# Moving the first layer's large loads behind the first placements of queries in a one-core transformer kernel

## What is computed

```python
xn = _layernorm(x)
# latent attention
q = xn @ wq ; k_lat = xn @ wk_down ; v_lat = xn @ wv_down
k = k_lat @ wk_up ; v = v_lat @ wv_up
y = softmax(causal(q @ k.T * 128**-0.5)) @ v ; a = y @ wo
# six layers
for i in range(6):
    h = attn_layer(shift_tokens(h), Wqkv[i], q_scale[i], k_scale[i], Wo[i]) + h
    h = ffn_layer(shift_tokens(h), ln_g[i], ln_b[i], W1[i], b1[i], W2[i], b2[i]) + h
out = x + a + h          # h starts as xn
```

## Time and profile before

| | us |
|---|---|
| median of 3 runs | 1826.56 (1821.57 to 1828.48) |
| the profiled execution, own time | 1832.16 |
| its span, first to last instruction | 1830.4 |
| TensorE busy | 1633.6 (89%) |
| VectorE busy | 1517.1 (83%) |
| ScalarE busy | 1312.9 (72%) |
| GpSimd busy | 1311.1 (72%) |
| mean granted TensorE clock | 0.975 |

### The profile page before, as it was taken

One profiled execution on the slowest core, in us unless ns is written; L12 is line 12 of the kernel. 1 busy time (PEld: TensorE's weight loads), 2 busy tenths in 40 slices (PEclk: granted clock), 3 DMA queues, 4 the chain that ended last, 5 costly groups with the idle time before them and its releaser, 6 DMA issues.

```text
span 1830.4 us, 72588 instructions
## 1 busy us (share of the span) xinstructions
PE 1633.6 (89%) x31192; PEld 1112.7 (61%) x31192; DVE 1517.1 (83%) x1941; ACT 1312.9 (72%) x1868; POOL 1311.1 (72%) x1287
## 2 busy tenths in 40 slices
PE   6777776788999999999999999999999999999995
PEld 5555665455656666666566666656666666666654
DVE  4466566689988999889899989989899998999973
ACT  2465564567788778777877887778777877887773
POOL 3100001888998888898789988889988899888871
PEclk7899999999999999999999999999999999999998
DMA  6011010010000100000100001000010000000000
GB/s 189 11 37 43 17 36 1 4 56 7 8 14 7 56 8 7 11 15 30 33 8 12 15 7 56 7 10 15 8 39 25 7 12 15 7 7 8 7 7 27
DMA packets 47997, 40.61 MB, mean 22 GB/s; under 512 B 33217, under 2 KB 41153, under 8 KB 46017
## 3 DMA queue, kind: packets, MB, share of 16 engines
q1 hardware_dynamic: 47680, 35.98, 7.0%
HBM read 20.22 MB, written 1.05 MB: 12 GB/s over the span
## 4 chain that ended last, share of the span: by engine, by line
PE 44%; issue 24%; DVE 17%; ACT 7%; POOL 6%; SPq 1%; DMA 0%; DVEq 0%; POOLq 0%; ACTq 0%
PE banks L1170 18%; PE banks L1444 10%; PE banks L1393 5%; PE banks L1468 5%; PE banks L1429 4%; DVE arena L1033 3%; DVE lnx L1095 3%; DVE small L1062 2%; DVE small L1068 2%; DVE small L1056 2%; DVE small L1080 1%; ACT L821 1%; ACT arena L755 1%; DVE arena L1028 1%; ACT L824 1%
## 5 line engine op out<-in xcount | busy, mean ns | idle before, releaser
L1444 PE MATMUL banks<-M,xs 128*32 128x512 f32 x3072 | 368.2, 597 | 0.6 <-ACT arena L755 0.3
L1028 DVE TENSOR_TENSOR arena<-banks,tabs 128x1024 f32<-128x1024 f32 x192 | 233.7, 1217 | 39.6 <-ACT arena L715 23.9
L514 POOL TENSOR_TENSOR arena<-arena 128x1024 f32<-128x1024 f32 x96 | 229.7, 2392 | 46.0 <-DVE arena L1033 45.7
L755 ACT ACTIVATE arena<-banks 128x1024 f32<-128x1024 f32 x192 | 196.9, 1025 | 71.1 <-PE banks L1444 69.8
L1033 DVE TENSOR_TENSOR arena<-banks,tabs 128x1024 f32<-128x1024 f32 x192 | 233.0, 1213 | 0.0
L519 POOL TENSOR_TENSOR arena<-arena 128x1024 f32<-128x1024 f32 x96 | 228.1, 2376 | 0.0
L509 POOL TENSOR_TENSOR prob<-prob,small 128x1024 f32<-128x1024 f32 x96 | 183.8, 1914 | 31.5 <-DVE small L1070 31.5
L1095 DVE SCALAR_TENSOR_TENSOR lnx<-lns,small 128x128 f32<-128x128 f32 x96 | 174.4, 1816 | 34.5 <-POOL small L562 33.5
L1170 PE MATMUL banks<-qkH,xsH 128*128 128x512 f32 x384 | 172.8, 450 | 32.3 <-DVE arena L1033 26.5
L1468 PE MATMUL banks<-arena 128*32 128x128 f32 x6144 | 192.3, 278 | 4.2 <-ACT arena L821 4.2
L574 POOL TENSOR_TENSOR arena<-arena,small 128x1024 f32<-128x1024 f32 x96 | 182.8, 1904 | 9.8 <-POOL arena L519 0.5
(11 more groups left out here) (127 smaller groups left out, 3727.0 us busy)
## 6 DMA issues: line engine op xcount, KB each, us to landing
arena<-in_wvo_dram SPq DMA_DIRECT2D x6, 1024.0 KB, 5.3
qkraw<-in_wqk_dram SPq DMA_DIRECT2D x6, 1024.0 KB, 5.3
gq<-w1w SPq DMA_DIRECT2D x64, 64.0 KB, 2.0
lns<-Xt SPq DMA_DIRECT2D x96, 32.0 KB
lns<-Xt SPq DMA_DIRECT2D x96, 31.8 KB
xsH<-w1w SPq DMA_DIRECT2D x32, 64.0 KB, 2.0
xsL<-w1w SPq DMA_DIRECT2D x32, 64.0 KB, 2.0
W<-in_w_dram SPq DMA_DIRECT2D x6, 341.0 KB, 3.2
```

Of the source, the lines that this page charges most:

```text
L514: pool.tensor_tensor(kc, kc, ks, ALU.add).then_inc(s["k_add"], 1)
L755: act.activation(vw[:, (2 * k + g) % RV, :], two(V_BANK), ACT.Copy).then_inc(s[f"v_cp{g}"], 1)
L1028: dve.tensor_tensor(heads(c), heads(two(0)), table(k % NT, kind), ALU.mult).then_inc(s[done], 1)
L1444: ins = pe.matmul(bk(V_BANK + z)[WIN * q:WIN * (q + 1), :], xs[:, b, t0:t0 + WIN], M[:, q, :, :].rearrange("p m n -> p (m n)"), start=True ...
```

## The change

The seven issues for layer 0 (`WVO0`, `qkraw`, scales, `tabc`, W1, W2, parameters) move behind `place_queries(0, 0)`, with its two waits and 16 DMAs. The table load comes after the scales now. The loads of W2 and of the parameters of layer 1 move behind `place_queries(0, 1)`. The other 6 calls of `place_queries` stay as they are, and so do the streams of the other four engines.

```diff
--- before.py
+++ after.py
@@ -321,8 +321,6 @@
             sp.dma_start(gwv, wvd).then_inc(lat_w, 16)
             sp.dma_start(gwo, wo.rearrange("(h p) n -> p h n", p=P)).then_inc(lat_w, 16)
             sp.dma_start(gwvu, wvuT).then_inc(lat_w, 16)
-            sp.dma_start(WVO0, wvo[0]).then_inc(wvo_in, 16)
-            sp.dma_start(tabc[:, :, :], tab_d).then_inc(tab_in, 16)
 
             def load_qk(l):
                 sp.dma_start(qkraw[:, :, :], wqk[l]).then_inc(qk_in, 16)
@@ -353,14 +351,6 @@
                 ahead_row = Xt[P - 1:P, n - 1, 64:D] if n % NT else zrow[:, :]
                 sp.dma_start(lns[0:1, f, 64:D], ahead_row).then_inc(rows_in[f], 16)
                 sp.dma_start(lns[:, f, 0:64], Xt[:, n, 0:64]).then_inc(rows_in[f], 16)
-
-            load_qk(0)
-            load_scales(0)
-            load_w1(0)
-            load_w2(0)
-            load_w2(1)
-            load_par(0)
-            load_par(1)
 
             def place_queries(it, z):
 
@@ -375,7 +365,18 @@
                         sp.dma_start(gQ[h][LAT * o:LAT * (o + 1), CH * z:CH * (z + 1)].bitcast(F32), part[LAT * h:LAT * (h + 1), :].bitcast(F32))\
                           .then_inc(gQ_in[h], 16)
 
-            for it in range(B * KV):
+            place_queries(0, 0)
+            sp.dma_start(WVO0, wvo[0]).then_inc(wvo_in, 16)
+            load_qk(0)
+            load_scales(0)
+            sp.dma_start(tabc[:, :, :], tab_d).then_inc(tab_in, 16)
+            load_w1(0)
+            load_w2(0)
+            load_par(0)
+            place_queries(0, 1)
+            load_w2(1)
+            load_par(1)
+            for it in range(1, B * KV):
                 for z in range(2):
                     place_queries(it, z)
             out_t = out.rearrange("b (t p) d -> p (b t) d", p=P)
```

## The result

The changed kernel takes 1846.87 us at the median of 4 runs (1841.94 to 1850.21), the kernel before 1827.52 in 4 runs, three of which are those that the forecast started from. The ratio is 1.0107, with a 95% interval of 1.0071 to 1.0143: slower by 1.1%, where 1844.1 us and +17.5 us had been forecast and 1837 to 1851 was the range. Timed again, 6 runs beside 17 of the kernel before, it was 1847.14 against 1829.99, ratio 1.0107 (1.0080 to 1.0134).

A forecast was written before the change was run, and what follows sets the result against it. The start follows its own chain of work: SyncE awaits the queries, TensorE runs in program order. First score +18.0 us, less 0.5 given back, is +17.5: 1826.56 + 17.5 = 1844.1 us, range 1837 to 1851.

The forecast's parts named there:

- What bounds the start: SyncE idles from 13.7 to 19.21 us awaiting the queries; earlier loads cost placements nothing at issue, only at landing.
- Placements: SyncE's first 16 placements still start no earlier than 19.21 us; their issue takes 10.3 us instead of 11.2.
- T0: Time when SyncE is free to issue WVO0: 29.5 us (29.2 to 30.4), where before it was issued at 9.00.
- The loads: From WVO0's issue until layer 0's parameters land: 13.0 us, bounds 12.2 and 14.5; landed at 42.5.
- TensorE: Products end at 40.0, hidden under the loads by 2.5 us; shifts take 2.3; first score at 44.8, +18.0 us.
- Given back: ScalarE's copy of the second query half no longer waits for placements: -0.5 us of the 0.96.
- GpSimd: Its preparation with tables and projection weights ends near 50 us, before a 243 us wait; costs nothing.
- The sum: Whole kernel: 18.0 - 0.5 = +17.5 us (16.4 to 19.9), 1844.1 us against the median, 1.0% slower.
- A: Rival: TensorE's clock rises sooner after the late start; price -7, giving +10.5, 1837.1 us; chance 0.10.
- B: Rival: loads land later or TensorE's clock stays lower; +19.9 to +22.4, 1849.0, up to 1851; chance 0.08.
- C: Rival: TensorE's scores overtake products and shifts, first score at 23.9; -3.4, 1823.2 us; chance 0.02.
- D: Rival: a resource with its own time sets later stages, so the end stays; 0 to -1, 1826; chance 0.02.

The follow-up runs named there:

- the run with its wait for placements: Changed kernel with WVO0, W1 and layer 0 parameters issued first and shifts(0) behind the first row's transposes: 1831.37 us against 1829.99, ratio 1.0006.
- half the dose: Changed kernel with only 8 placements (heads 0 and 1) ahead of the seven loads, those of heads 2 and 3 behind: 1848.86 us in one run.

## Why the prediction was right

*What bounds the start.* Right: SyncE's first placement stayed at 19.13, and no load had held it. That the loads ahead cost the placements something at landing (2.4 us at the median) is true of some, but not of the last, for which the copy waited: it landed in 1.98.

*Placements.* 10.1 us of issue instead of 10.3, T0 at 29.29 instead of 29.5. The reason given, a queue without loads, was not the right one: the 11.2 us of before come mostly from one issue of 1.45 us, and such an issue appears with the needed loads first too, when no load is left in the queue. Why it is absent in both profiles of the changed kernel is open.

*The loads.* The parameters landed at 32.79 + 8.65 = 41.4, that is 12.15 us after T0. The sum had 13.0 with bounds of 12.2 and 14.5. This was the term that was mis-sized most, by 0.85 us; the lower bound, made of loads one behind the other, was the true value. Nothing lay beside them. The upper end was the value with placements beside them: 14.0 and 14.2 us to the release in the two runs that have it.

*TensorE.* Right: `WVO0` landed at 34.5 (34.8), the products ended at 38.04 + 2.08 = 40.1 (40.0) and were covered, by 1.45 us instead of 2.5, since the load was shorter. The run with only the needed loads late showed what is behind the cover. From shifts to first score 2.27 us (2.3). First score +17.07 (18.0). The idle time began at 18.3 and not at 19.5, since `products(0, 0)`, which was part of the group at 16.64, left it with the change; that cost nothing. The sum comes out of two figures as well: `WVO0` started 20.3 us later, and the shifts started 12.3 us after its issue where they had started 15.5 us after it, so 3.2 us had been slack: 20.3 - 3.2 = 17.1.

*Given back.* 0.47 us (0.5), whole at the second block of transposes too: 49.87 - 43.84 = 6.03 us after the first score, 33.26 - 26.77 = 6.49 before. *GpSimd:* nothing (nothing), its split ended at 49.9 (near 50).

*The sum.* +16.83 at the first projection in the first profile, +20.5 in the second, +17.2 and +19.4 between medians, forecast +17.5. The forecast's 1844.1 lies 2.8 us below the 1846.87: 1.0 of it is the kernel before, at 1827.52 instead of the 1826.56 of the three runs that the forecast started from, and 1.8 is the difference. In the comparison with more runs it is the other way round: the kernel before is 3.4 us higher (1829.99) and the difference 0.3 smaller. That the medians agree so closely with +17.5 is in part luck, with runs of one kernel spread over some 13 us.

*The rivals.* A, the clock that rises sooner, did happen, but it was worth nothing in the end. In the kernel before the clock stayed at the lower level until 43.5, 16.7 us after the first score. In the changed kernel it was up from 49.6 us, 5.8 us after the first score, and down again at 53.0:

```profile
50.00:51.00 1.00, 1.00 (x8) 0.96 (x9) 0.26 (x1) 0.67 (x3) 0.87 (x2) 1.00 0.00 0
...
54.00:55.00 1.00, 1.00 (x7) 1.00 (x6) 0.00 (x0) 0.00 (x0) 0.00 (x0) 0.50 0.39 96
```

The last figures are the granted clock, the DMA's share and GB/s. The first of the products with the values, in the kernel before and in the changed kernel:

```profile
37.68 3.68 PE L1170 MATMUL banks<-arena 128*128 128x64 f32 x16 [1.70 <-DVE arena L949]
```

```profile
53.19 3.67 PE L1171 MATMUL banks<-arena 128*128 128x64 f32 x16 [1.80 <-DVE arena L950]
```

There the changed kernel was only 53.19 - 37.68 = 15.5 us late, 1.1 us less than at the second block of transposes (49.87 - 33.26 = 16.6). It lost this again in the next 25 us, in which its clock was at the upper level for less time: at the next 512-column products, 60.17 before and 76.86 after, it was 16.7 us late. Over the whole attention stage the pair differs by 0.24 us, so the price of -7 was far too high, and the bound of 9.4 us too: at its widest the stage moved by 5.8 us between executions, 278.4 to 284.2, without the run with its wait for placements.

B fell with the loads' 12.15 us. C fell visibly: TensorE stood idle for 16.29 us with the queries of heads 0 and 1 placed by about 26 us, and nothing passed the products. The Trainium skill (TensorE: Matmul & The Clock Gate, Part 3) says that matmuls start and end in program order. This trace agrees, with a load missing, which the trace of before could not show. D fell with the first projection at +16.83.

`products` took 2.08 us after the idle time, at the lower of the two levels, and the mean granted clock from 22 to 49 us was 0.51; the kernel before had its second product at the same level after 3.1 us without a matmul. The Trainium skill (TensorE: Matmul & The Clock Gate, Part 1) has the half rate as the state after idleness, and both traces agree.

## What to carry to other kernels

Before moving a load behind something, find the first instruction on each engine that waits for it, and what stands behind that instruction in the engine's order. Here the products and the shifts, which stand ahead of the first score, needed three of the seven loads, 1.37 MB; the other loads, issued near 100 us, still had 180 us to spare. The cost was the time by which the loads started later, 20.3 us, less the 3.2 us that they had had to spare, and all but 0.5 us of it showed at the end of the attention stage, since nothing in between had slack of its own.

A DMA queue that is idle, or an issuing engine that waits, is worth loads: from 13.7 to 19.2 us SyncE had nothing to do, and starting the loads only after that was about half of the loss (8.8 of 17.1 us at the first score), before a single placement stood in front of them. If small transfers come late, look at their issue: 16 at 0.63 us took 10 to 11 us on one engine and 5.4 on two.

## What had not been expected

Small transfers inside one core, issued while large loads are still queued, cost the last loads 1.7 to 2.0 us (12.3 and 12.4 us to the release without them in the two profiles of the changed kernel, 14.0 and 14.2 with them) and land late themselves: 7.1 us at the median and 9.4 at most, instead of 2.0.

Single DMA issues of 1.2 to 1.7 us turn up among issues of 0.59 us, in five of the twelve profiles, once in each among the first 16 placements, between 26 and 29 us. With 16 issues in a row on the path one of these is 10% of the stretch; what causes them was not tried.

The same kernel's attention stage differed by 3.4 us between two executions, and its granted clock with it (0.94 and 0.93). An early gain from the clock, 1.1 us here, can be gone 25 us later. A delay of this size is read better from the time of one landmark in the trace, set against another that no edit touches, than from single run times: of the single runs, one with half the dose was slower than the changed kernel's median.
